# An adaLN block in float32 on one core: where the feed-forward takes its 64-row half block

## The chip, the cores and the metric

The kernel runs on 1 core of a Trainium2 chip. The metric is the device time of one execution in microseconds (us), lower is better. Three runs of the kernel before took 1242.53, 1242.93 and 1243.69 us; the median is 1242.93.

## What is computed

For each of 8 batches of 512 tokens with 1024 features, the reference computes (cut to what matters):

```python
mod = (silu(c) @ wmod)                      # shifts, scales and gates sa, ca, ga, sb, cb, gb
h = layernorm(x) * (1 + ca) + sa
x = x + ga * gelu(h @ ((w1.T @ w2.T) * sparse_mask) + b2)
h = layernorm(x) * (1 + cb) + sb
P = h @ U1                                  # 1024 -> 256
H = P @ V1 + b1                             # 256 -> 2 x 2752
act = silu(H[:, :2752]) * H[:, 2752:]       # gate half, up half
Z = act @ U2                                # 2752 -> 256
x = x + gb * (Z @ V2 + b2_ffn)              # 256 -> 1024
```

ga and gb are the gates, kept at a size of at least 0.25. All of it is in float32; the kernel splits each operand of a large product into a high and a low part and adds three products (hi x hi, hi x lo, lo x hi).

## The kernel before

It works in two passes. The first (until about 440 us) computes the modulation, the sparse attention-like product, the second normalisation and P, batch by batch, and stores x and P in HBM. The second pass is the feed-forward, one batch after the other, and the change is in it alone.

**Blocks.** The 2752 hidden features are taken in IB = 22 blocks: 21 of 128 and one of 64 (`width[-1]`, the half block). All five engines have their order written out by hand; semaphores tie them together. `three` (L498 to L500) issues the three matmuls of a split product. For a full block i TensorE computes

- the gate product (`gate_product`, 2 x 3 matmuls of 512 columns, into PSUM bank i % 2),
- the up product (`up_product`, as many, into bank 2 + i % 2),
- and, two blocks later, Z (`z_product`, 2 x 3 matmuls that add to banks 4 and 5).

For the half block, gate and up share one product of 6 matmuls (64 rows each in one bank). Its Z has only 64 rows to sum over, so the two column halves of U2 lie on different partitions and their matmuls run side by side on two halves of the array: 6 matmuls at L804, in three pairs, each a 64*128 tile of the array where all others are 128*128.

**Between the products.** ACT applies the silu (`silu`, L996) and writes the high part (`act_hi_part`, L1007; for the half block L1006 writes a second copy on the other 64 partitions first). DVE multiplies by up (`multiply`, L1285) and writes the low part (`act_lo_part`, L1295; for the half block L1293 first). ACT's order is silu of block i, then `act_hi` of block i - 1. DVE's is multiply of i, then `act_lo` of i - 1. Z of block i waits on `act_lo_ready`. The next gate product waits until the block before the last has been multiplied (`act_done`).

**The end of a batch.** TensorE's `batch` is

```python
            for i in range(2, IB):
                h_product(b, q, i)
                z_product(b, q, i - 2)
            if not last:
                gate_product(b + 1, 1 - q, 0)
            z_product(b, q, IB - 2)
            z_product(b, q, IB - 1)
            if not last:
                up_product(b + 1, 1 - q, 0)
                h_product(b + 1, 1 - q, 1)
            out_product(b)
```

so the next batch's first products lie between the last ones of this batch. After the last Z, ACT and DVE split Z (L1031, L1305) and the output product (`out_product`, 48 matmuls) follows. In the last batch there are no such products of a next batch.

**The V2 split.** V2 times the gate is split once per batch: ACT writes `v_hi` (L1014) in four parts, one after each of the `act_hi` parts of positions 12 to 15 (17 to 20 in batch 0), and GpSimd the four parts of `v_lo` (L1411) behind them.

**SP** issues all DMAs: P of the next batch behind a wait on `gate_done`, V2 and the broadcast gates behind waits on `v2_lo_ready` and `x2_biased`, and the output tiles and the next x tiles behind `out_ready`.

Of the kernel before, what the change touches and what calls it, by code (L numbers as in the profile page):

```python
# [30 lines left out]
ACT = mybir.ActivationFunctionType  # L31
ALU = mybir.AluOpType
AX = mybir.AxisListType

P = 128
# [4 lines left out]
def adaln_block(nc, x, w1, w2t, b2, mask, u1, v1, u2, v2, b1_main, b1_tail, b2f, ct, wmod, out):  # L40
    NB, TOK, D = x.shape
# [36 lines left out]
    with ExitStack() as ctx:  # L78
# [6 lines left out]
        bank = ctx.enter_context(nc.psum_tensor("bank", [P, 8, HALF], F32))  # L85


        b1_sb = buf(ctx, "b1_sb", [P, IB, 2])
# [68 lines left out]
        v1_hi = buf(p2, "v1_hi", [P, RB, 2 * INTER], F32R)  # L157
        v1_lo = buf(p2, "v1_lo", [P, RB, 2 * INTER], F32R)
# [8 lines left out]
        act = buf(p2, "act", [P, 2, TOK])  # L167
# [78 lines left out]
        gate_done = sem("gate_done")  # L246
# [44 lines left out]
        def at_start(b, early=True):  # L291

            return isinstance(b, int) and b == 0 and early
# [53 lines left out]
        BAND_ORDER = [6, 7] + list(range(6))  # L347
        V2_PARTS = [(r, slice(h * HALF, (h + 1) * HALF)) for r in range(RB) for h in range(NH)]
        V2_FROM = [17] + [12] * (NB - 1)

        block = ctx.enter_context(nc.Block())

# [142 lines left out]
        def _(pe):  # L495
# [252 lines left out]
            iteration(NB - 1, True, True, False)  # L748


            def h_waits(b, q, i):
                if i == 0:
                    pe.wait_ge(pt_in[q], (b - q) * 8 + 16)
                if not at_start(b, i < 2):
                    pe.wait_ge(act_done, b * IB + i - 1)

            def h_part(q, i, acc, name, v_hi, v_lo):
                if i % 4 == 0 or i == IB - 1:
                    pe.wait_ge(w_ready, piece_of[name, i // 4])
                for r in range(RB):  # L760
                    last = three(acc, v_hi[:, r], v_lo[:, r], pt[:, q, 0, r, :], pt[:, q, 1, r, :],
                                 r == 0, r == RB - 1)
                return last

            def gate_product(b, q, i):
                cols = slice(i * P, i * P + P)
                h_waits(b, q, i)
                h_part(q, i, bank[:, i % 2, :], "gate", v1_hi[:, :, cols], v1_lo[:, :, cols]).then_inc(gate_done, 1)

            def up_product(b, q, i):  # L770
                cols = slice(UP + i * P, UP + i * P + P)
                h_part(q, i, bank[:, 2 + i % 2, :], "up", v1_hi[:, :, cols], v1_lo[:, :, cols]).then_inc(up_done, 1)

            def h_product(b, q, i):

                if i < IB - 1:
                    gate_product(b, q, i)
                    up_product(b, q, i)
                else:
                    h_waits(b, q, i)  # L780
                    cols = slice(i * P, i * P + P)
                    h_part(q, i, bank[:, i % 2, :], "up", v1_hi[:, :, cols], v1_lo[:, :, cols]).then_inc(gate_done, 1)

            def z_product(b, q, i):
                pe.wait_ge(act_lo_ready, b * IB + i + 1)
                if i % 4 == 0:
                    pe.wait_ge(w_ready, piece_of["u2", i // 4])
                if at_start(b, i == 0):
                    pe.wait_ge(gb_ready, 1)
                elif i == 0:  # L790
                    pe.wait_ge(z_lo_ready, b * 2)
                w = width[i]
                slot = (q * IB + i) % 4
                if w == P:
                    for r in range(RB):
                        cols = slice(r * P, (r + 1) * P)
                        last = three(bank[:, 4 + r, :], u2_hi[:, i, cols], u2_lo[:, i, cols],
                                     act_hi[:, slot, :], act_lo[:, slot, :], i == 0, False)
                else:
                    terms = ((u2_hi, act_hi), (u2_hi, act_lo), (u2_lo, act_hi))  # L800
                    for t, (weight, moving) in enumerate(terms):
                        for r in range(RB):
                            rows = slice(r * w, (r + 1) * w)
                            last = nc.tensor.matmul(bank[:, 4 + r, :], weight[rows, i, r * P:(r + 1) * P],  # L804
                                                    moving[rows, slot, :], start=False, stop=t == len(terms) - 1)
                last.then_inc(z_step, 1)

            def out_product(b):
# [55 lines left out]
        def _(ae):  # L864
# [123 lines left out]
            iteration(NB, False, True, False)  # L988


            def silu(b, q, i):
                w = width[i]
                ae.wait_ge(gate_done, b * IB + i + 1)
                if not at_start(b, i < 2):
                    ae.wait_ge(act_lo_ready, b * IB + i - 1)
                nc.scalar.activation(act[0:w, i % 2, :], bank[0:w, i % 2, :], ACT.Silu,  # L996
                                     bias=b1_sb[0:w, i, 0:1]).then_inc(silu_done, 1)

            def act_hi_part(b, q, i):
                w = width[i]  # L1000
                slot = (q * IB + i) % 4
                ae.wait_ge(act_done, b * IB + i + 1)
                if not at_start(b, i < 4):
                    ae.wait_ge(z_step, b * IB + max(i - 3, 0))
                if w < P:
                    nc.scalar.activation(act_hi[w:P, slot, :], act[0:w, i % 2, :], ACT.Copy)  # L1006
                nc.scalar.activation(act_hi[0:w, slot, :], act[0:w, i % 2, :], ACT.Copy).then_inc(act_hi_ready, 1)  # L1007

            def v2_hi_part(b, part):
                r, cols = V2_PARTS[part]  # L1010
# [31 lines left out]
        def _(dve):  # L1042
# [229 lines left out]
            nc.vector.tensor_tensor(gbb2_rows, gb_rows[:], b2f_rows, ALU.mult).then_inc(gbb2_ready, 1)  # L1272


            def multiply(b, q, i):

                w = width[i]
                if w == P:
                    up = bank[0:w, 2 + i % 2, :]
                    dve.wait_ge(up_done, b * (IB - 1) + i + 1)  # L1280
                else:
                    up = bank[P - w:P, i % 2, :]
                    dve.wait_ge(gate_done, b * IB + i + 1)
                dve.wait_ge(silu_done, b * IB + i + 1)
                nc.vector.scalar_tensor_tensor(act[0:w, i % 2, :], up, b1_sb[0:w, i, 1:2],  # L1285
                                               act[0:w, i % 2, :], ALU.add, ALU.mult).then_inc(act_done, 1)

            def act_lo_part(b, q, i):
                w = width[i]
                slot = (q * IB + i) % 4  # L1290
                dve.wait_ge(act_hi_ready, b * IB + i + 1)
                if w < P:
                    nc.vector.tensor_tensor(act_lo[w:P, slot, :], act[0:w, i % 2, :], act_hi[0:w, slot, :],  # L1293
                                            ALU.subtract)
                nc.vector.tensor_tensor(act_lo[0:w, slot, :], act[0:w, i % 2, :], act_hi[0:w, slot, :],  # L1295
                                        ALU.subtract).then_inc(act_lo_ready, 1)

            def batch(b, q, last):
# [174 lines left out]
```

## Time and profile before

| | |
|---|---|
| median of three runs | 1242.93 us |
| the profiled execution: its time / its span | 1241.24 / 1239.5 us |
| busy: TensorE, weight load | 1186.1 us (96%), 950.3 us (77%) |
| busy: DVE, ACT, GpSimd | 669.8 (54%), 407.0 (33%), 314.9 us (25%) |
| granted TensorE clock, mean of the execution | 0.988 of full |
| HBM traffic over the span | 133 GB/s |

The span is the time between the first and last instruction of the profiled execution. Engines are PE (TensorE matmuls), PEld (its weight loads), DVE, ACT, POOL (GpSimd) and SP. A row of the timeline gives start and duration in us; matmuls overlap, so the distance of two starts tells more than the duration. In brackets stands how long the engine had been idle before and whose result ended that. The granted clock is 1.00 at 2.4 GHz and 0.50 at 1.2 GHz. In such rows x2 after a shape counts two instructions.

### The profile page before, as it was taken

Reading aid. Unit: us, or ns where it says so; the run is one execution under the profiler, and the core shown is the slowest. Engines: PE = TensorE matmul, PEld = TensorE weight load, DVE = VectorE, ACT = ScalarE, POOL = GpSimd, SP = SyncE. Lnnn points to the kernel's source line nnn. Section 1 sums busy time; section 2 is a strip of 40 time slices with the busy share of each in tenths; the row PEclk is TensorE's granted clock in tenths of the full one; section 3 lists DMA queues with packets and bytes.
Section 4 is the critical chain, followed back from the end, with each engine's and each line's share of the span. In section 5 each row is a group of like instructions: output and inputs, shape, how many; then the busy total and the mean of one; then the engine's idle time right before and its main releaser. Section 6 shows DMA issues by size and latency. Waiting matters only on the chain.

```text
span 1239.5 us, 15161 instructions
## 1 busy us (share of the span) xinstructions
PE 1186.1 (96%) x5617; PEld 950.3 (77%) x5617; DVE 669.8 (54%) x1049; ACT 407.0 (33%) x684; POOL 314.9 (25%) x257
## 2 busy tenths in 40 slices
PE   7788999999999899999999999999999999999997
PEld 4446678877786678888888888888888888888885
DVE  0838699999996643543444443443444444344343
ACT  0122334444443264413322323322332332332331
POOL 0023221332313176541211302203113122131110
PEclk9898999999999899999999999999999999999999
DMA  9796635535457454240131122104015014013001
GB/s 350 290 371 250 270 145 196 226 146 211 165 199 288 172 172 162 95 156 15 68 119 52 68 77 93 68 25 145 11 58 170 1 68 140 31 68 119 18 1 68
DMA packets 54145, 165.76 MB, mean 134 GB/s; under 512 B 4992, under 2 KB 9536, under 8 KB 52032
## 3 DMA queue, kind: packets, MB, share of 16 engines
q1 hardware_dynamic: 54080, 164.86, 36.3%
q8 instruction: 44, 0.72, 0.2%
q14 instruction: 21, 0.17, 0.0%
HBM read 122.84 MB, written 42.01 MB: 133 GB/s over the span
## 4 chain that ended last, share of the span: by engine, by line
PE 82%; DVE 9%; ACT 2%; issue 2%; DMA 2%; POOL 1%; SPq 1%; DVEq 0%; ACTq 0%
PE bank L498 25%; PE bank L500 24%; PE bank L499 24%; PE bank L568 4%; DVE nrm L1070 2%; PE bank L664 2%; DMA x<-in_x 2%; PE bank L533 2%; DVE bn L1228 1%; DVE h_lo L1171 1%; DVE bn L1060 1%; DMA wm_sb<-in_wmod 1%; POOL g L1349 1%; PE bank L804 1%; DVE xr L1223 1%
## 5 line engine op out<-in xcount | busy, mean ns | idle before, releaser
L1285 DVE SCALAR_TENSOR_TENSOR act<-bank,b_sb,act 128x512 f32<-128x512 f32 (+1 forms) x176 | 131.9, 750 | 382.4 <-PE bank L500 360.7
L996 ACT ACTIVATE act<-bank,b_sb 128x512 f32<-128x512 f32 (+1 forms) x176 | 121.1, 689 | 505.7 <-PE bank L500 504.5
L498 PE MATMUL bank<-pt,v_hi 128*128 128x512 f32 x688 | 268.7, 391 | 1.5 <-DVE act L1285 1.5
L499 PE MATMUL bank<-pt,v_hi 128*128 128x512 f32 x688 | 267.7, 389 | 0.0
L500 PE MATMUL bank<-pt,v_lo 128*128 128x512 f32 x688 | 267.7, 389 | 0.0
L1295 DVE TENSOR_TENSOR act_lo<-act,act_hi 128x512 fp32r<-128x512 f32 (+1 forms) x176 | 164.9, 937 | 0.2
L498 PEld LDWEIGHTS bank<-pt,v_hi 128*128 128x128 f32 x688 | 129.1, 188 | 31.2 <-issue 2.6
L500 PEld LDWEIGHTS bank<-pt,v_lo 128*128 128x128 f32 x688 | 129.2, 188 | 27.0
L499 PEld LDWEIGHTS bank<-pt,v_hi 128*128 128x128 f32 x688 | 129.2, 188 | 26.3
L1421 POOL TENSOR_TENSOR x2t<-gbb_bc,x2t 128x512 f32<-128x512 f32 x64 | 85.5, 1358 | 241.3 <-DMA x2t<-x_dram 241.3
L498 PE MATMUL bank<-act_hi,u_hi 128*128 128x512 f32 x336 | 130.8, 389 | 0.9 <-DVE act_lo L1295 0.9
L499 PE MATMUL bank<-act_lo,u_hi 128*128 128x512 f32 x336 | 130.7, 389 | 0.0
L500 PE MATMUL bank<-act_hi,u_lo 128*128 128x512 f32 x336 | 130.7, 389 | 0.0
L889 ACT ACTIVATE h_hi<-bank,now 128x512 fp32r<-128x512 f32 x128 | 84.6, 687 | 113.8 <-PE bank L568 113.6
L1171 DVE SCALAR_TENSOR_TENSOR h_lo<-bank,now,h_hi 128x512 fp32r<-128x512 f32 x128 | 92.7, 745 | 33.2 <-ACT h_hi L889 32.7
L1007 ACT ACTIVATE act_hi<-act 128x512 fp32r<-128x512 f32 (+1 forms) x176 | 109.5, 622 | 0.4 <-DVE act L1285 0.3
L1411 POOL TENSOR_TENSOR v_lo<-v2g,v_hi 128x512 fp32r<-128x512 f32 x32 | 41.4, 1295 | 244.1 <-ACT v_hi L1014 244.1
L1349 POOL TENSOR_TENSOR g<-g,now_ga 128x512 f32<-128x512 f32 x64 | 74.5, 1173 | 69.7 <-ACT g L894 61.8
L568 PE MATMUL bank<-ident,nrm 128*128 128x128 f32 x480 | 71.4, 282 | 12.6 <-DVE nrm L1070 9.0
L568 PEld LDWEIGHTS bank<-ident,nrm 128*128 128x128 f32 x480 | 57.2, 145 | 24.7 <-DVE h_lo L1171 8.7
L498 PE MATMUL bank<-h_hi,attn_hi 128*128 128x512 f32 x176 | 73.4, 417 | 2.5 <-DVE mod_sum L1133 2.2
L498 PEld LDWEIGHTS bank<-act_hi,u_hi 128*128 128x128 f32 x336 | 63.1, 188 | 14.4 <-DVE act_lo L1295 1.3
(122 smaller groups left out, 1600.2 us busy)
## 6 DMA issues: line engine op xcount, KB each, us to landing
wm_sb<-in_wmod SPq DMA_DIRECT2D x10, 2048.0 KB, 11.1
xr<-in_x SPq DMA_DIRECT2D x16, 1024.0 KB, 6.8
x_dram<-xr SPq DMA_DIRECT2D x16, 1024.0 KB, 4.2
x2t<-x_dram SPq DMA_DIRECT2D x32, 512.0 KB, 4.0
out<-x2t SPq DMA_DIRECT2D x32, 512.0 KB, 4.9
xs<-in_x SPq DMA_DIRECT2D x7, 2048.0 KB, 7.7
pt_dram<-pt_st SPq DMA_DIRECT2D x8, 1024.0 KB, 3.9
pt<-pt_dram SPq DMA_DIRECT2D x8, 1024.0 KB, 5.8
```

The lines of the kernel that those rows point to most:

```text
L498: nc.tensor.matmul(acc, s_hi, m_hi, start=start, stop=False)
L499: nc.tensor.matmul(acc, s_hi, m_lo, start=False, stop=False)
L500: return nc.tensor.matmul(acc, s_lo, m_hi, start=False, stop=stop)
L568: last = nc.tensor.transpose(bank[:, 2 + k % 2, n * P:(n + 1) * P], src[:, n, k * P:(k + 1) * P], ident[:])
L889: nc.scalar.activation(h_hi[:, k, :], bank[:, 2 + k % 2, :], ACT.Copy, scale=scale[:, k:k + 1]).then_inc(hi_ready, 1)
L996: nc.scalar.activation(act[0:w, i % 2, :], bank[0:w, i % 2, :], ACT.Silu, bias=b1_sb[0:w, i, 0:1]).then_inc(silu_done, 1)
L1007: nc.scalar.activation(act_hi[0:w, slot, :], act[0:w, i % 2, :], ACT.Copy).then_inc(act_hi_ready, 1)
L1171: nc.vector.scalar_tensor_tensor(h_lo[:, k, :], bank[:, 2 + k % 2, :], scale[:, k:k + 1], h_hi[:, k, :], ALU.mult, ALU.subtract).then_inc( ...
L1285: nc.vector.scalar_tensor_tensor(act[0:w, i % 2, :], up, b1_sb[0:w, i, 1:2], act[0:w, i % 2, :], ALU.add, ALU.mult).then_inc(act_done, 1)
L1295: nc.vector.tensor_tensor(act_lo[0:w, slot, :], act[0:w, i % 2, :], act_hi[0:w, slot, :], ALU.subtract).then_inc(act_lo_ready, 1)
L1349: nc.gpsimd.tensor_tensor(g[:, t, :], g[:, t, :], now_ga[:, t:t + 1].to_broadcast([P, TOK]), ALU.mult).then_inc(g_ready, 1)
L1421: nc.gpsimd.tensor_tensor(half, gbb2_bc[:, h * HALF:(h + 1) * HALF], half, ALU.add).then_inc(x2_biased, 1)
```

## The change

From batch 1 on, the half block is taken as the twelfth of 22: blocks 0 to 10, then block 21 (the half one), then 11 to 20. Batch 0 keeps the old order, since its weights arrive in that order. The functions of the three computing engines now get a position j and look up the block in `BLOCKS[b][j]`. Buffers and banks (j % 2, the slot of `act_hi`) and all semaphore counts go by position; weights and bias columns by block. `up_done` counts only full blocks, so its target comes from `whole_blocks`. The flag that closes the accumulation of Z moves to the last position.

```diff
+        BLOCKS = [list(range(IB))] + [list(range(IB // 2)) + [IB - 1] + list(range(IB // 2, IB - 1))] * (NB - 1)
+
+        def whole_blocks(b, j):
+            return b * (IB - 1) + sum(width[i] == P for i in BLOCKS[b][:j + 1])
...
-            def h_product(b, q, i):
-
-                if i < IB - 1:
-                    gate_product(b, q, i)
-                    up_product(b, q, i)
+            def h_product(b, q, j):
+                i = BLOCKS[b][j]
+                if width[i] == P:
+                    gate_product(b, q, j)
+                    up_product(b, q, j)
                 else:
-                    h_waits(b, q, i)
+                    h_waits(b, q, j)
...
-            def z_product(b, q, i):
-                pe.wait_ge(act_lo_ready, b * IB + i + 1)
+            def z_product(b, q, j):
+                i = BLOCKS[b][j]
+                pe.wait_ge(act_lo_ready, b * IB + j + 1)
...
-                                     act_hi[:, slot, :], act_lo[:, slot, :], i == 0, False)
+                                     act_hi[:, slot, :], act_lo[:, slot, :], j == 0, j == IB - 1)
...
-                    dve.wait_ge(up_done, b * (IB - 1) + i + 1)
+                    dve.wait_ge(up_done, whole_blocks(b, j))
```

`silu`, `act_hi_part`, `multiply` and `act_lo_part` change in the same way. The new lines shift line numbers: L804 becomes L812, L1285 becomes L1295, L1293 and L1295 become L1303 and L1305, L996 becomes L1006, L1006 and L1007 become L1016 and L1017, L498 to L500 become L503 to L505.

How the order of instructions moves is seen best at three places.

DVE at the end of batch 2, before (L1285 multiply, L1293 and L1295 `act_lo`, L1305 the split of Z):

```order
L1285 SCALAR_TENSOR_TENSOR act<-bank,b_sb,act 128x512
L1295 TENSOR_TENSOR act_lo<-act,act_hi 128x512
L1285 SCALAR_TENSOR_TENSOR act<-bank,b_sb,act 64x512
L1295 TENSOR_TENSOR act_lo<-act,act_hi 128x512
L1293 TENSOR_TENSOR act_lo<-act,act_hi 64x512
L1295 TENSOR_TENSOR act_lo<-act,act_hi 64x512
L1305 TENSOR_TENSOR z_lo<-bank,z_hi 128x512 x2
```

and now:

```order
L1295 SCALAR_TENSOR_TENSOR act<-bank,b_sb,act 128x512
L1305 TENSOR_TENSOR act_lo<-act,act_hi 128x512
L1295 SCALAR_TENSOR_TENSOR act<-bank,b_sb,act 128x512
L1305 TENSOR_TENSOR act_lo<-act,act_hi 128x512 x2
L1315 TENSOR_TENSOR z_lo<-bank,z_hi 128x512 x2
```

The two 64-row subtracts are gone from the end; two full ones stand behind a full multiply.

ACT in the middle of a batch, where the half block arrives, now (L1006 silu, L1016 and L1017 `act_hi`, L1024 `v_hi`):

```order
L1006 ACTIVATE act<-bank,b_sb 64x512
L1017 ACTIVATE act_hi<-act 128x512
L1006 ACTIVATE act<-bank,b_sb 128x512
L1016 ACTIVATE act_hi<-act 64x512
L1017 ACTIVATE act_hi<-act 64x512
L1024 ACTIVATE v_hi<-v2g 128x512
L1006 ACTIVATE act<-bank,b_sb 128x512
```

The two 64-row copies come just ahead of the first `v_hi`, in the place of one full copy.

TensorE in the middle of a batch, now: the last matmuls of the up product of position 13, the Z of the half block (L812) and the start of the gate product of position 14, with the semaphores waited on:

```order
L503 MATMUL bank<-pt,v_hi 128x512
L504 MATMUL bank<-pt,v_hi 128x512
L505 MATMUL bank<-pt,v_lo 128x512
L812 MATMUL bank<-act_hi,u_hi 128x512 [waits act_lo_ready]
L812 MATMUL bank<-act_hi,u_hi 128x512
L812 MATMUL bank<-act_lo,u_hi 128x512 x2
L812 MATMUL bank<-act_hi,u_lo 128x512 x2
L503 MATMUL bank<-pt,v_hi 128x512 [waits act_done]
```

Before, these six stood behind the Z of block 20 and ahead of the next batch's up product, at L804.

## Rows read from the trace of the kernel before

**Rows 1.** The page: busy us of each engine, share of the span, instructions.

```profile
PE 1186.1 (96%) x5617; PEld 950.3 (77%) x5617; DVE 669.8 (54%) x1049; ACT 407.0 (33%) x684; POOL 314.9 (25%) x257
```

**Rows 2.** Waits from 540 us on: who waited for whom, total us, times, longest.

```profile
PEld bank L804 <- DVE act_lo L1295: 5.1, 7, 0.9
...
PE bank L804 <- DVE act_lo L1295: 2.1, 7, 0.5
```

**Rows 3.** Timeline, end of batch 2: start us, us, engine, line, operation [idle before].

```profile
722.24 0.68 DVE L1295 TENSOR_TENSOR act_lo<-act,act_hi 64x512 fp32r<-64x512 f32 x1
722.31 0.39 PE L500 MATMUL bank<-act_hi,u_lo 128*128 128x512 f32 x1
...
722.98 0.50 PE L804 MATMUL bank<-act_hi,u_hi 64*128 64x512 f32 x2 [0.28 <-DVE act_lo L1295]
...
723.55 0.40 PE L804 MATMUL bank<-act_hi,u_lo 64*128 64x512 f32 x2
...
723.88 0.50 PE L498 MATMUL bank<-pt,v_hi 128*128 128x512 f32 x1
...
724.22 0.40 PE L499 MATMUL bank<-pt,v_hi 128*128 128x512 f32 x1
```

**Rows 4.** Timeline, TensorE at the end of batch 1.

```profile
623.60 0.49 PE L804 MATMUL bank<-act_hi,u_hi 64*128 64x512 f32 x2 [0.28 <-DVE act_lo L1295]
```

**Rows 5.** Timeline, end of the last batch: TensorE, ACT and DVE.

```profile
1211.50 0.69 ACT L996 ACTIVATE act<-bank,b_sb 128x512 f32<-128x512 f32 x1 [2.87 <-PE bank L500]
...
1213.80 0.39 PE L500 MATMUL bank<-act_hi,u_lo 128*128 128x512 f32 x1
...
1215.16 0.39 PE L500 MATMUL bank<-pt,v_lo 128*128 128x512 f32 x1
...
1215.58 0.69 ACT L996 ACTIVATE act<-bank,b_sb 64x512 f32<-64x512 f32 x1 [2.87 <-PE bank L500]
...
1216.17 0.62 ACT L1007 ACTIVATE act_hi<-act 128x512 fp32r<-128x512 f32 x1
...
1216.37 0.75 DVE L1285 SCALAR_TENSOR_TENSOR act<-bank,b_sb,act 64x512 f32<-64x512 f32 x1 [2.16 <-ACT act L996]
...
1217.05 0.68 DVE L1295 TENSOR_TENSOR act_lo<-act,act_hi 128x512 fp32r<-128x512 f32 x1
...
1217.15 0.63 ACT L1006 ACTIVATE act_hi<-act 64x512 fp32r<-64x512 f32 x1 [0.37 <-DVE act L1285]
...
1217.78 0.50 PE L498 MATMUL bank<-act_hi,u_hi 128*128 128x512 f32 x1 [0.87 <-DVE act_lo L1295]
...
1220.47 0.39 PE L804 MATMUL bank<-act_hi,u_lo 64*128 64x512 f32 x2
...
1222.88 0.50 PE L498 MATMUL bank<-v_hi,z_hi 128*128 128x512 f32 x1 [2.02 <-DVE z_lo L1305]
```

**Rows 6.** Timeline, first pass: TensorE goes to the 32-column form (L533) without a wait.

```profile
372.95 0.39 PE L500 MATMUL bank<-h_hi,attn_lo 128*128 128x512 f32 x1
...
373.27 1.92 PE L533 MATMUL bank<-xs,c_pad 128*32 128x512 f32 x16
```

**Rows 7.** Timeline, batch 1: GpSimd's `v_lo` and DVE's subtract beside it.

```profile
584.36 1.30 POOL L1411 TENSOR_TENSOR v_lo<-v2g,v_hi 128x512 fp32r<-128x512 f32 x1 [24.38 <-ACT v_hi L1014]
...
584.59 1.62 DVE L1295 TENSOR_TENSOR act_lo<-act,act_hi 128x512 fp32r<-128x512 f32 x1
```

**Rows 8.** Windows: us, busy PE, PEld, DVE, ACT, POOL, granted clock, DMA share, GB/s.

```profile
720.00:725.00 5.00, 4.72 (x23) 3.31 (x23) 2.54 (x5) 2.84 (x5) 0.00 (x0) 1.00 0.00 0
```

**Rows 9.** Window of the last output product, and two of its matmuls in the timeline.

```profile
1224.00:1225.00 1.00, 1.00 (x4) 0.80 (x3) 0.00 (x0) 0.00 (x0) 0.00 (x0) 0.50 0.00 0
...
1223.68 0.53 PE L498 MATMUL bank<-v_hi,z_hi 128*128 128x512 f32 x1
...
1227.33 0.39 PE L498 MATMUL bank<-v_hi,z_hi 128*128 128x512 f32 x1
```

More of the change, by code:

```diff
@@ L748, in _, with h_waits @@
             iteration(NB - 1, True, True, False)
-            def h_waits(b, q, i):
-                if i == 0:
+            def h_waits(b, q, j):
+                if j == 0:
                     pe.wait_ge(pt_in[q], (b - q) * 8 + 16)
-                if not at_start(b, i < 2):
-                    pe.wait_ge(act_done, b * IB + i - 1)
+                if not at_start(b, j < 2):
+                    pe.wait_ge(act_done, b * IB + j - 1)
             def h_part(q, i, acc, name, v_hi, v_lo):
@@ L804, in z_product @@
                             last = nc.tensor.matmul(bank[:, 4 + r, :], weight[rows, i, r * P:(r + 1) * P],
-                                                    moving[rows, slot, :], start=False, stop=t == len(terms) - 1)
+                                                    moving[rows, slot, :], start=False,
+                                                    stop=j == IB - 1 and t == len(terms) - 1)
                 last.then_inc(z_step, 1)
@@ L988, in _, with silu, act_hi_part @@
             iteration(NB, False, True, False)
-            def silu(b, q, i):
+            def silu(b, q, j):
+                i = BLOCKS[b][j]
                 w = width[i]
[L993 to L996, printed above, removed]
+                ae.wait_ge(gate_done, b * IB + j + 1)
+                if not at_start(b, j < 2):
+                    ae.wait_ge(act_lo_ready, b * IB + j - 1)
+                nc.scalar.activation(act[0:w, j % 2, :], bank[0:w, j % 2, :], ACT.Silu,
                                      bias=b1_sb[0:w, i, 0:1]).then_inc(silu_done, 1)
[L999 to L1004, printed above, removed]
+            def act_hi_part(b, q, j):
+                w = width[BLOCKS[b][j]]
+                slot = (q * IB + j) % 4
+                ae.wait_ge(act_done, b * IB + j + 1)
+                if not at_start(b, j < 4):
+                    ae.wait_ge(z_step, b * IB + max(j - 3, 0))
                 if w < P:
-                    nc.scalar.activation(act_hi[w:P, slot, :], act[0:w, i % 2, :], ACT.Copy)
-                nc.scalar.activation(act_hi[0:w, slot, :], act[0:w, i % 2, :], ACT.Copy).then_inc(act_hi_ready, 1)
+                    nc.scalar.activation(act_hi[w:P, slot, :], act[0:w, j % 2, :], ACT.Copy)
+                nc.scalar.activation(act_hi[0:w, slot, :], act[0:w, j % 2, :], ACT.Copy).then_inc(act_hi_ready, 1)
             def v2_hi_part(b, part):
@@ L1272, in _, with multiply, act_lo_part @@
             nc.vector.tensor_tensor(gbb2_rows, gb_rows[:], b2f_rows, ALU.mult).then_inc(gbb2_ready, 1)
-            def multiply(b, q, i):
+            def multiply(b, q, j):
+                i = BLOCKS[b][j]
                 w = width[i]
                 if w == P:
-                    up = bank[0:w, 2 + i % 2, :]
-                    dve.wait_ge(up_done, b * (IB - 1) + i + 1)
-                else:
[L1282 to L1291, printed above, removed]
+                    up = bank[0:w, 2 + j % 2, :]
+                    dve.wait_ge(up_done, whole_blocks(b, j))
+                else:
+                    up = bank[P - w:P, j % 2, :]
+                    dve.wait_ge(gate_done, b * IB + j + 1)
+                dve.wait_ge(silu_done, b * IB + j + 1)
+                nc.vector.scalar_tensor_tensor(act[0:w, j % 2, :], up, b1_sb[0:w, i, 1:2],
+                                               act[0:w, j % 2, :], ALU.add, ALU.mult).then_inc(act_done, 1)
+            def act_lo_part(b, q, j):
+                w = width[BLOCKS[b][j]]
+                slot = (q * IB + j) % 4
+                dve.wait_ge(act_hi_ready, b * IB + j + 1)
                 if w < P:
-                    nc.vector.tensor_tensor(act_lo[w:P, slot, :], act[0:w, i % 2, :], act_hi[0:w, slot, :],
+                    nc.vector.tensor_tensor(act_lo[w:P, slot, :], act[0:w, j % 2, :], act_hi[0:w, slot, :],
                                             ALU.subtract)
-                nc.vector.tensor_tensor(act_lo[0:w, slot, :], act[0:w, i % 2, :], act_hi[0:w, slot, :],
+                nc.vector.tensor_tensor(act_lo[0:w, slot, :], act[0:w, j % 2, :], act_hi[0:w, slot, :],
                                         ALU.subtract).then_inc(act_lo_ready, 1)
```

20 lines of the change are left out of this document (11 added, 9 removed).

## The prediction

> **What bounds the kernel now.** I read the page first: TensorE is busy for 1186.1 of 1239.5 us, the other engines for 54% or less [rows 1]. The change touches the feed-forward's batches 1 to 7 alone, from 540 us on. There the list of waits has only two entries that repeat and in which TensorE is the one that waits, both at L804, the product of the 64-row block: seven times, once a batch, for `act_lo` [rows 2]. Everything else in that list is another engine waiting for TensorE. So a saving on TensorE's queue in this stage comes through one for one, and a delay on ACT or DVE costs nothing until it holds a matmul back.
>
> The unit of the sum is one matmul of 512 columns. A full block has 18 (6 gate, 6 up, 6 Z), and 18 matmuls after one silu comes the next, 4.08 us on (1211.50 to 1215.58) [rows 5], so a **slot** is 4.08/18 = 0.227 us. A matmul's row is 0.39 long because matmuls overlap; what counts is the distance of starts. In the half block, the hidden product takes 6 slots and Z 3, since two 64-row matmuls run side by side (x2 in one row).
>
> What to see in [rows 3]: the end of a batch as it is. The last matmul of Z(20) starts at 722.31, so the next is due at 722.54. But L804 needs the second half of `act_lo`, which DVE starts at 722.24 and ends at 722.92; L804 starts at 722.98, 0.44 late. The next start is 0.34 behind it, 0.11 more than a slot (after any break the first row is 0.50 long, not 0.39). Leaving the two-tile form, 723.55 to 723.88 is 0.33 (0.10 over), and 723.88 to 724.22 again 0.34 (0.11 over). Sum: 0.44 + 0.11 + 0.10 + 0.11 = **0.76 us per batch over its slots**. Cross-check: from one L804 to the next is 722.98 - 623.60 = 99.38 us [rows 3, 4]; a batch has 21 x 18 + 9 + 48 (output) = 435 slots, 98.60 us, which leaves 0.78.
>
> The last batch has no next batch's products as cover [rows 5]. From 1213.80 (last start of Z(18)) to 1220.47 (last pair of Z(21)) are 6.67 us for 21 slots (4.76): **1.91 us over**. Z(20) waits too, because `act_hi`(20) stands on ACT behind the silu of the short block and `act_lo`(20) on DVE behind its multiply. Then Z is split and the output product starts at 1222.88.
>
> **The change, part by part.** No instruction is added or removed; 7 of 8 batches (1 to 7) take the half block as their twelfth, and a full one last. Slots, bytes, DMAs and the numbers of ACT and DVE operations stay. Batch 0 keeps its order and its 0.76.
>
> 1. *Wait at the end of batches 1 to 6.* With a full block last, its up product ends 18 slots (Z(19), the next gate, Z(20)), 4.08 us, before its Z is due. From the last start of up to a usable `act_lo`, by the steps of [rows 5]: 0.42 to DVE's start, 0.78 to `act_hi`, 0.65 more (0.62 and the signal), 0.68 subtract, 0.06 to TensorE = 2.6 us. It fits by 1.5, and Z(20) by more. Removed: the whole 0.76, as no form switch is left there either.
>
> 2. *The switch of form is not removed but moved.* In the middle, nothing waits (part 3), but the array still goes from 128-row to 64-row matmuls and back. The way out is read above, 0.10 + 0.11. The way in without a wait is not in the feed-forward. The nearest row is the switch to the 32-column form in the first pass, where no engine is waited for [rows 6]: 372.95 to 373.27 is 0.32, 0.09 over. I take 0.09 + 0.11 for the way in; together 0.41 us per batch. Bounds: from below 0 (the switch is hidden by weights loaded ahead), from above the 0.44 + 0.11 of today, if what looks like a wait were the switch. I take the value of [rows 6], as the idle of L804 is put down to DVE and the 0.06 from the end of `act_lo` to the start fits a signal.
>
> The Trainium skill, "TensorEngine Tiling (Array Packing)", under "Key Properties", says that a change of tiling mode (not of tile) drains TensorE. By a full drain the next matmul would start 0.39 behind the last, 0.16 over instead of 0.09, and the sum below would be about 0.5 us smaller over seven batches. The row at 373.27, 0.32 behind its predecessor, speaks against the full price, though not against the rule.
>
> Saved in batches 1 to 6: 0.76 - 0.41 = 0.35 each, **2.1 us**.
>
> 3. *Does the wait come back in the middle?* Take T as the last start of the short hidden product. ACT runs silu, then `act_hi` of the block before; DVE multiply at T + 1.21. The next silu is due only when the next gate is complete, 12 slots on: T + 2.72 + 0.42 = 3.14, and both `act_hi` halves follow by 5.0. DVE starts the next multiply at T + 4.50 (18 slots and 0.42) and the two `act_lo` halves at 5.2 and 5.9, done by 6.6. TensorE wants them after 36 slots, T + 8.16. One thing crosses: the V2 split begins at this very position, and where GpSimd computes `v_lo` a DVE subtract takes 1.62 instead of 0.68 [rows 7]. Even with both halves at 1.62 the chain ends at 5.2 + 3.2 = 8.4, and the first pair is due at T + 8.39 plus 0.09. So: nothing, at worst 0.1. Z of the block before the half block has 18 slots between the end of the short product and its own start, as in any step. SP's order is unchanged: its waits on `gate_done` 22 per batch count the same, and `v2_lo` comes 6 slots earlier in the batch, before loads that are used a batch later.
>
> 4. *The last batch.* With G the last start of the last block's gate: silu at G + 0.42, `act_hi`(20) done at G + 1.63; up's last start G + 1.36, multiply at G + 1.78, `act_lo`(20) from G + 2.46 to 3.14 (0.68 behind the multiply's start, as 1217.05 behind 1216.37), Z(20) at G + 3.19. It is due 13 slots on, at G + 2.95: 0.24 late, and 0.11 for the restart. `act_lo`(21) is ready by G + 4.0, Z(21) due at 4.7: no wait. Over slots: 0.35 at the end and 0.41 in the middle, 0.76 for 1.91 today. Saved: **1.15 us**. Behind it the chain is the same: last start of Z to first output matmul 2.41 us.
>
> Sum: 2.1 + 1.15 = 3.25, say **3.2 us less**. The profiled execution has a span of 1239.5 and a time of 1241.24; its span would be 1236.3. The median of the runs shown is 1242.93, 1.7 above, and the forecast goes from it: **1239.7 us**. About 0.2% (2.5 us) is what a measurement of this kernel can tell from no change.
>
> **Rivals.**
> - *The way in costs in the middle what it costs now* (0.44 + 0.11). Then batches 1 to 6 save nothing and the last 1.91 - 0.35 - 0.76 = 0.8: 1242.1 us. For it: the waits are 2.1 us over seven with 0.5 as the longest [rows 2], so they hardly differ from batch to batch, as a fixed price would. Against it: [rows 6], and that a chain of ACT and DVE steps of fixed length is as even.
> - *The low clock goes too.* In the last output product the granted clock falls from 2.4 to 1.2 GHz after TensorE had been idle for 2.0 us and, before that, in two breaks of 0.9 [rows 5] and 0.5 [rows 2]; the window from 1224 shows 0.50 [rows 9]. Nine starts from 1223.68 take 3.65 us instead of 2.04, which costs 1.6. The change takes most of the two earlier breaks away and leaves the 2.0. If the fall needs them: 3.2 + 1.6 = 4.8 less, 1238.1 us. I hold it unlikely, as the longest break stays.
> - *A wait takes the place at the batch's end*: the last full block comes later than the short one, and if GpSimd is at work there each subtract takes 1.62. In batches 1 to 6 this would cost at most 0.1, and in the last batch, where Z(20) would come at G + 4.1, 1.3 late with its restart, it leaves next to nothing (1.91 - 1.45 - 0.41), since Z(21) would be 0.15 late as well. With 2.1 - 0.6 from the others some 1.6 less, 1241.3 us. Against it: in the 5 us around the end of batch 2 GpSimd does nothing [rows 8].
> - *Slower*: the half block meets the V2 split in the middle, ACT and DVE fall behind and TensorE waits at L804 there, where it costs 0.35 per batch before anything is lost. It decides when the chain of part 3 ends later than T + 8.8; for 2.5 us of loss it must end 0.8 us past the due time in all seven batches, at T + 9.3: 1245.4 us. Rows give 8.4 at worst.
>
> **How the numbers follow.** Forecast 0.62 (its own range 1238.9 to 1240.6, of which about 0.07 falls within 0.2%), way in at today's price 0.14, clock 0.12, wait at the end 0.08, slower 0.04. Faster by over 0.2%, that is under 1240.4: 0.55 + 0.12 = 0.67. Within: 0.07 + 0.14 + 0.08 = 0.29. Slower: 0.04. The range of 8 in 10 is 1238.0 to 1242.0: it ends just past the clock case and just short of the first rival, and leaves out the slow case and about half of each of those two (0.04 + 0.06 + 0.07). The bounds of the way in are its bounds too: free, it would save 7 x 0.2 more (1238.3); at today's price it is the first rival.
>
> **What would show it.** Right: L804 in batches 1 to 7 without idle put down to DVE, its first start about 0.32 behind the matmul before it; 99.03 us from one batch to the next where it was 99.38; one late Z(20) of about 0.24 in the last batch; 2.0 us of idle before the output product still there. Wrong: the distance of 0.67 stays at L804 in the middle (first rival), a clock of 1.00 throughout the last 20 us (second), idle before Z(20) in batches 1 to 6 (third), or over 0.7 us at L804 (fourth).

## The result, and the profile after

| | before | changed |
|---|---|---|
| median, 9 runs each | 1242.6 us (1241.32 to 1243.69) | 1239.13 us (1238.01 to 1239.99) |
| profiled execution: time / span | 1241.24 / 1239.5 us | 1238.43 / 1236.6 us |
| TensorE busy | 1186.1 us | 1185.6 us |

The ratio is 0.9971, with a 95% interval of 0.9960 to 0.9981. That is 3.5 us less, with an interval of some 2.4 to 5.0. It is 0.29% faster; the weak end of the interval, 0.19%, lies just short of the 0.2% that the prediction set as its line. Forecast were 3.2 us less, 1239.7 us.

The waits from 540 us on, in the changed kernel (who waited for whom, total us, times, longest). They answer to [rows 2]:

```profile
DVE z_lo L1315 <- ACT z_hi L1041: 26.5, 7, 3.9
...
ACT act L1006 <- DVE act_lo L1305: 15.0, 7, 2.4
...
PEld bank L812 <- issue: 2.5, 7, 0.4
...
PE bank L503 <- DVE z_lo L1315: 2.0, 1, 2.0
...
PEld bank L503 <- DVE act_lo L1305: 0.5, 1, 0.5
```

The half block's Z (now L812) waits for nobody any more in batches 1 to 7: its weight load is put down to "issue". The 2.0 us ahead of the last output product are still there.

TensorE in the middle of batch 1 and of batch 2:

```profile
586.55 0.39 PE L505 MATMUL bank<-pt,v_lo 128*128 128x512 f32 x1
586.87 0.50 PE L812 MATMUL bank<-act_hi,u_hi 64*128 64x512 f32 x2
587.20 0.40 PE L812 MATMUL bank<-act_lo,u_hi 64*128 64x512 f32 x2
587.44 0.39 PE L812 MATMUL bank<-act_hi,u_lo 64*128 64x512 f32 x2
587.76 0.50 PE L503 MATMUL bank<-pt,v_hi 128*128 128x512 f32 x1
588.10 0.40 PE L504 MATMUL bank<-pt,v_hi 128*128 128x512 f32 x1
...
685.90 0.50 PE L812 MATMUL bank<-act_hi,u_hi 64*128 64x512 f32 x2
```

The way in is 0.32 (586.55 to 586.87) where it was 0.67 in [rows 3]; then 0.33, 0.24, 0.32 and 0.34. The five distances make 1.55 us; five slots are 1.13, so the visit (into the 64-row form and out again) costs 0.42 us. From L812 to L812 are 685.90 - 586.87 = 99.03 us, where [rows 3, 4] had 99.38.

ACT and DVE around the half block in batch 2:

```profile
683.41 1.68 DVE L1305 TENSOR_TENSOR act_lo<-act,act_hi 64x512 fp32r<-64x512 f32 x1
...
685.19 0.69 ACT L1006 ACTIVATE act<-bank,b_sb 128x512 f32<-128x512 f32 x1 [2.10 <-DVE act_lo L1305]
...
686.01 0.75 DVE L1295 SCALAR_TENSOR_TENSOR act<-bank,b_sb,act 128x512 f32<-128x512 f32 x1 [0.92 <-PE bank L505]
```

GpSimd works beside the second half's subtract (its `v_lo` starts at 683.16 and takes 1.39), and the subtract takes 1.68 us and ends at 685.09; the pair is at 685.90. The silu of position 13 waits for that subtract, since it overwrites the same `act` buffer, and starts some 0.5 us late; DVE's next multiply at 686.01 still waits for TensorE alone, so nothing is lost.

The end of a full batch, batch 2: no break in TensorE's queue, with the last Z product and the next batch's up product a slot apart. Z(21) starts at 722.29, and the last `act_lo` was ready at 720.56.

```profile
719.08 1.48 DVE L1305 TENSOR_TENSOR act_lo<-act,act_hi 128x512 fp32r<-128x512 f32 x2
...
722.29 0.39 PE L503 MATMUL bank<-act_hi,u_hi 128*128 128x512 f32 x1
...
723.42 0.39 PE L505 MATMUL bank<-act_hi,u_lo 128*128 128x512 f32 x1
723.65 0.39 PE L503 MATMUL bank<-pt,v_hi 128*128 128x512 f32 x1
```

And the last batch (it answers to [rows 5]):

```profile
1210.44 0.39 PE L505 MATMUL bank<-act_hi,u_lo 128*128 128x512 f32 x1
...
1214.52 0.39 PE L505 MATMUL bank<-act_hi,u_lo 128*128 128x512 f32 x1
1214.99 0.50 PE L503 MATMUL bank<-act_hi,u_hi 128*128 128x512 f32 x1
1215.34 0.40 PE L504 MATMUL bank<-act_lo,u_hi 128*128 128x512 f32 x1
...
1217.66 0.39 PE L505 MATMUL bank<-act_hi,u_lo 128*128 128x512 f32 x1
1220.06 0.50 PE L503 MATMUL bank<-v_hi,z_hi 128*128 128x512 f32 x1 [2.01 <-DVE z_lo L1315]
```

Z(20) starts at 1214.99 where 1214.75 was due, 0.24 late, with 0.12 for the restart; Z(21) follows without a gap. The output product starts 2.40 us behind the last start of Z, as before (2.41).

**The stretch.** Runs of one kernel differ by a us or two, and much of that arises ahead of batch 1, where only two of the versions below, all_batches and halves, differ from the others (the first matmul after batch 0's output product starts at 540.20 before and 540.54 now). So below I also compare the *stretch*: from that matmul's start to the last matmul's start. The changed kernel was traced twice (changed_again, part 4): the spans are 1236.6 and 1235.6 us, the stretches 691.92 and 691.93. All others but full_rows were traced once.

In the kernel before:

```profile
540.20 0.39 PE L498 MATMUL bank<-pt,v_hi 128*128 128x512 f32 x1
...
1235.28 0.39 PE L500 MATMUL bank<-v_hi,z_lo 128*128 128x512 f32 x1
```

In the changed kernel:

```profile
540.54 0.39 PE L503 MATMUL bank<-pt,v_hi 128*128 128x512 f32 x1
...
1232.46 0.39 PE L505 MATMUL bank<-v_hi,z_lo 128*128 128x512 f32 x1
```

695.08 us before, 691.92 now: 3.16 us less, for 3.25 in the sum of the prediction. Both include the fall of the clock at the end (part 4).

### The profile page after: what moved, and what is told of

The parts are those of the page before. It is cut to its first block, busy times and chain, and to the rows that moved or that the text cites. A ratio compares the mean times of both kernels' runs of the same rounds, so it can differ in the third digit from the quotient of the medians.

```text
span 1236.6 us, 15161 instructions
## 1 busy us (share of the span) xinstructions
PE 1185.6 (96%) x5617; PEld 950.3 (77%) x5617; DVE 666.6 (54%) x1049; ACT 408.4 (33%) x684; POOL 316.9 (26%) x257
## 4 chain that ended last, share of the span: by engine, by line
PE 84%; DVE 8%; DMA 2%; issue 2%; ACT 1%; SPq 1%; POOL 1%; DVEq 0%; ACTq 0%
PE bank L503 25%; PE bank L505 25%; PE bank L504 25%; PE bank L573 4%; DVE nrm L1080 2%; PE bank L669 2%; PE bank L538 2%; DMA x<-in_x 2%; DVE bn L1238 1%; DVE h_lo L1181 1%; DVE bn L1070 1%; DMA wm_sb<-in_wmod 1%; POOL g L1359 1%; DVE xr L1233 1%; PE bank L812 1%
## 5 line engine op out<-in xcount | busy, mean ns | idle before, releaser
L1295 DVE SCALAR_TENSOR_TENSOR act<-bank,b_sb,act 128x512 f32<-128x512 f32 (+1 forms) x176 | 132.0, 750 | 372.8 <-PE bank L505 349.8
L1006 ACT ACTIVATE act<-bank,b_sb 128x512 f32<-128x512 f32 (+1 forms) x176 | 121.2, 690 | 495.2 <-PE bank L505 478.9
L503 PE MATMUL bank<-pt,v_hi 128*128 128x512 f32 x688 | 269.1, 391 | 1.5 <-DVE act L1295 1.5
L505 PE MATMUL bank<-pt,v_lo 128*128 128x512 f32 x688 | 268.0, 390 | 0.0
L1305 DVE TENSOR_TENSOR act_lo<-act,act_hi 128x512 fp32r<-128x512 f32 (+1 forms) x176 | 161.6, 918 | 0.9
L503 PEld LDWEIGHTS bank<-pt,v_hi 128*128 128x128 f32 x688 | 129.2, 188 | 31.5 <-DVE act L1295 4.1
L505 PEld LDWEIGHTS bank<-pt,v_lo 128*128 128x128 f32 x688 | 129.2, 188 | 26.6
L503 PE MATMUL bank<-act_hi,u_hi 128*128 128x512 f32 x336 | 131.0, 390 | 0.1
L505 PE MATMUL bank<-act_hi,u_lo 128*128 128x512 f32 x336 | 130.9, 390 | 0.0
L1017 ACT ACTIVATE act_hi<-act 128x512 fp32r<-128x512 f32 (+1 forms) x176 | 109.8, 624 | 7.0 <-DVE act L1295 6.9
L503 PE MATMUL bank<-h_hi,attn_hi 128*128 128x512 f32 x176 | 73.1, 415 | 2.5 <-DVE mod_sum L1143 2.2
L503 PEld LDWEIGHTS bank<-act_hi,u_hi 128*128 128x128 f32 x336 | 63.1, 188 | 13.6 <-DVE act_lo L1305 0.5
```

Source lines behind the costliest of these rows:

```text
L503: nc.tensor.matmul(acc, s_hi, m_hi, start=start, stop=False)
L505: return nc.tensor.matmul(acc, s_lo, m_hi, start=False, stop=stop)
L1006: nc.scalar.activation(act[0:w, j % 2, :], bank[0:w, j % 2, :], ACT.Silu, bias=b1_sb[0:w, i, 0:1]).then_inc(silu_done, 1)
L1017: nc.scalar.activation(act_hi[0:w, slot, :], act[0:w, j % 2, :], ACT.Copy).then_inc(act_hi_ready, 1)
L1295: nc.vector.scalar_tensor_tensor(act[0:w, j % 2, :], up, b1_sb[0:w, i, 1:2], act[0:w, j % 2, :], ALU.add, ALU.mult).then_inc(act_done, 1)
L1305: nc.vector.tensor_tensor(act_lo[0:w, slot, :], act[0:w, j % 2, :], act_hi[0:w, slot, :], ALU.subtract).then_inc(act_lo_ready, 1)
```

## The experiments

All stretches are worked out from such pairs of rows. A ratio is to executions of the kernel before that were timed together with that version; their median moved from 1241.5 to 1242.6 us, so the medians of different rows can't be compared closely.

| run | stretch, us | against changed | median, us | ratio to before, 95% interval |
|---|---|---|---|---|
| before | 695.08 | +3.16 | | |
| changed | 691.92, 691.93 | | 1239.13 | 0.9971 (0.9960 to 0.9981) |
| last_only | 694.03 | +2.11 | 1239.55 | 0.9984 (0.9975 to 0.9993) |
| inner_only | 693.00 | +1.08 | 1239.81 | 0.9986 (0.9977 to 0.9995) |
| three_switches | 697.75 | +5.83 | 1243.9 | 1.0016 (1.0007 to 1.0026) |
| full_rows | 692.06, 693.64 | see below | 1240.4, 1241.98 | one execution each |
| second_last | 692.49 | +0.57 | 1238.66 | 0.9974 (0.9963 to 0.9986) |
| fifth | 691.93 | +0.01 | 1238.98 | 0.9976 (0.9965 to 0.9986) |
| filled | 690.30 | -1.62 | 1236.52 | 0.9962 (0.9949 to 0.9976) |
| before_filled | 693.56 | +1.64 | 1240.35 | 0.9986 (0.9976 to 0.9996) |
| all_batches | 690.32 | -1.60 | 1237.53 | 0.9960 (0.9946 to 0.9974) |
| halves | 689.53 | -2.39 | 1237.02 | 0.9959 (0.9945 to 0.9973) |

**1. Which places give the gain?** Two kernels with one part of the change each. last_only:

```diff
-        BLOCKS = [list(range(IB))] + [list(range(IB // 2)) + [IB - 1] + list(range(IB // 2, IB - 1))] * (NB - 1)
+        BLOCKS = [list(range(IB))] * (NB - 1) + [list(range(IB // 2)) + [IB - 1] + list(range(IB // 2, IB - 1))]
```

> Theory (the gain is the sum of seven places): only the last batch gets the half block in its middle, so only its 1.15 us are saved against the kernel before, ratio about 0.999, span about 1238.3; batches 1 to 6 keep 99.38 us from one half block to the next. Rival (all of the gain comes out of the end of the program, where the chain is bare): nearly the whole 3.5 us, span about 1236.

inner_only:

```diff
-        BLOCKS = [list(range(IB))] + [list(range(IB // 2)) + [IB - 1] + list(range(IB // 2, IB - 1))] * (NB - 1)
+        BLOCKS = [list(range(IB))] + [list(range(IB // 2)) + [IB - 1] + list(range(IB // 2, IB - 1))] * (NB - 2) + [list(range(IB))]
```

> Theory: six times 0.35 = 2.1 us less than the kernel before, ratio about 0.9983, span about 1237.4; 99.03 us from one half block to the next in batches 1 to 6, and the last batch ends as before, with 1.91 us over its slots. Rival (gain only at the end of the program): no change.

Measured in the stretch: 695.08 - 694.03 = 1.05 us from the last batch, 695.08 - 693.00 = 2.08 us from the six others; together 3.13, the whole gain of 3.16. In last_only the old wait stands in batches 1 to 6 (six times; the last batch has none):

```profile
PE bank L812 <- DVE act_lo L1305: 1.7, 6, 0.3
```

The rival falls: batches 1 to 6 give two thirds. The timed ratios (0.9984 and 0.9986) each exclude 1 and cannot tell the two parts from each other; the stretch can. The span of last_only, 1239.1 us, was above the 1238.3 expected, as its first pass took 0.75 us more (540.95 against 540.20).

**2. What does a visit to the 64-row form cost?** three_switches takes the pairs apart:

```diff
                     for t, (weight, moving) in enumerate(terms):
+                        if b and t == 1:
+                            gate_product(b, q, j + 3)
+                        elif b and t == 2:
+                            up_product(b, q, j + 3)
...
                 for i in range(2, IB):
-                    h_product(b, q, i)
+                    if not (b and i == IB // 2 + 3):
+                        h_product(b, q, i)
                     z_product(b, q, i - 2)
```

> As the changed kernel, but the three pairs of 64-row matmuls in batches 1 to 7 stand apart, with the gate and the up product of the position after next between them: three visits to the 64-row form instead of one. Theory (a visit costs 0.41 us: 0.09 + 0.11 in, 0.10 + 0.11 out): two more visits per batch, 7 x 0.82 = 5.7 us more than the changed kernel, about 1244.9 us. Rival (the switch is nearly free and 0.41 was something else at the place): within 0.5 us of the changed kernel.

Its middle of batch 1:

```profile
587.15 0.39 PE L505 MATMUL bank<-pt,v_lo 128*128 128x512 f32 x1
587.47 0.50 PE L816 MATMUL bank<-act_hi,u_hi 64*128 64x512 f32 x2
587.90 0.50 PE L503 MATMUL bank<-pt,v_hi 128*128 128x512 f32 x1
588.23 0.39 PE L504 MATMUL bank<-pt,v_hi 128*128 128x512 f32 x1
```

A pair alone costs 0.32, 0.43 and 0.33, which is 1.08 for three slots (0.68): 0.40. Two more visits in seven batches cost 5.83 us, 0.42 each. The rival falls. The timed ratio, 1.0016, is slower than before: two more visits outweigh what the moved wait gives.

full_rows does without the form. It takes the weights of block 0 there, so it leaves the half block's right share out of Z, and serves for its times alone:

```diff
-                            rows = slice(r * w, (r + 1) * w)
-                            last = nc.tensor.matmul(bank[:, 4 + r, :], weight[rows, i, r * P:(r + 1) * P],
-                                                    moving[rows, slot, :], start=False,
+                            last = nc.tensor.matmul(bank[:, 4 + r, :], weight[:, 0, r * P:(r + 1) * P],
+                                                    moving[:, slot, :], start=False,
```

> As the changed kernel, but the Z of the half block is done with six 128-row matmuls, on weights of block 0 and all 128 rows of act, so the half block's share of Z is not what the reference asks for; there is no change of form. Theory: three more slots (0.68) and no visit to the 64-row form (0.41) per batch: 0.27 us more in each of batches 1 to 7, 99.30 us from batch to batch, 1.9 us more in the stretch from batch 1 to the end. Rival (a visit costs as much as the old wait and its breaks, 0.76): 0.1 us less per batch.

Its six matmuls in two batches:

```profile
588.40 0.39 PE L505 MATMUL bank<-pt,v_lo 128*128 128x512 f32 x1
588.63 0.62 PE L811 MATMUL bank<-act_hi,u_hi 128*128 128x512 f32 x2
...
687.91 0.62 PE L811 MATMUL bank<-act_hi,u_hi 128*128 128x512 f32 x2
```

The way in is 0.23, a plain slot, and from batch to batch are 687.91 - 588.63 = 99.28 us for 99.30 expected. So doing the half block side by side is worth 0.25 us net in each batch (99.28 - 99.03): 0.68 us for the three slots saved, less 0.42 for the visit. The stretch of this first run, 692.06, is not 1.9 longer than the changed kernel's but 0.14, and the reason is the clock (part 4).

**3. Does it have to be the middle?** second_last puts the half block at position 20, fifth at position 4:

```diff
+        BLOCKS = [list(range(IB))] + [list(range(IB - 2)) + [IB - 1, IB - 2]] * (NB - 1)
...
+        BLOCKS = [list(range(IB))] + [list(range(4)) + [IB - 1] + list(range(4, IB - 1))] * (NB - 1)
```

> The half block as the last but one of batches 1 to 7, not in the middle. Theory (what counts is how many slots lie between a block's hidden product and its Z): in batches 1 to 6 the Z of the half block is still covered (its act_lo ready at G + 3.9, the pair due at G + 4.3), so 99.03 us from batch to batch as with the middle; in the last batch the pair is due at G + 2.95 and 0.96 late, so 1.28 us over its slots at the end where the changed kernel has 0.76 in all: 0.5 us more than the changed kernel. Rival (it must stand in the middle, away from the end): batches 1 to 6 wait at the half block again, 2 us more than the changed kernel.

> The half block as the fifth of batches 1 to 7, away from the V2 split, which stays at positions 12 to 15. Theory (the split beside it costs nothing, as the pair was due 0.8 us after act_lo): the same stretch from batch 1 to the end as the changed kernel, 691.9 us, within 0.1. Rival (DVE's 1.68 us subtract beside GpSimd holds something back): up to 0.5 us less.

second_last: in batches 1 to 6 the pair stands 0.32 behind its predecessor (720.79 to 721.11), as in the middle. In the last batch it waits for `act_lo`:

```profile
1214.62 0.39 PE L505 MATMUL bank<-act_hi,u_lo 128*128 128x512 f32 x1
1215.90 0.50 PE L812 MATMUL bank<-act_hi,u_hi 64*128 64x512 f32 x2 [0.90 <-DVE act_lo L1305]
```

1.05 us late where 0.96 was worked out; the stretch is 0.57 longer than the changed kernel's, for 0.5. So what counts is how many slots lie between a block's hidden product and its Z, not the place as such, and only the last batch makes a difference. fifth: 691.93 against 691.92. The V2 split beside the half block costs nothing, and the rival (up to 0.5) falls.

**4. The clock at the end.** filled puts work into the idle, before_filled does so in the kernel before:

```diff
                     h_product(b + 1, 1 - q, 1)
+                else:
+                    for n in range(9):
+                        nc.tensor.matmul(bank[:, n % 2, :], v1_hi[:, 0, 0:P], pt[:, q, 0, 0, :],
+                                         start=True, stop=True)
                 out_product(b)
```

> As the changed kernel, with nine more matmuls of 512 columns into idle banks after the last Z of the last batch, where TensorE is idle for 2.0 us while Z is split; their results are not used. Theory (the fall of the clock follows from that idle): granted clock 1.00 through the last output product, 1.6 us less than the changed kernel, about 1237.5 us. Rival (the fall has another cause, or comes anyway): no change, clock 0.50 for some 3.4 us as before; if nine matmuls reach past the end of the split, up to 0.3 us more.

> The kernel before with nine unused matmuls in the 2.0 us of idle ahead of the last output product. Theory (this idle alone makes the clock fall; the breaks of 0.9 and 0.5 us ahead of it do not): granted clock 1.00 in the output product, 1.6 us less than before. Rival (the earlier breaks make it fall, in whole or in part): the clock falls all the same, no change.

Windows of the changed kernel (us, then busy PE, PEld, DVE, ACT, POOL, granted clock, DMA share, GB/s):

```profile
1221.00:1222.00 1.00, 1.00 (x4) 0.81 (x3) 0.00 (x0) 0.00 (x0) 0.00 (x0) 0.50 0.00 0
1222.00:1223.00 1.00, 1.00 (x4) 0.81 (x3) 0.51 (x1) 0.00 (x0) 0.00 (x0) 0.50 0.00 0
1223.00:1224.00 1.00, 1.00 (x4) 0.71 (x4) 0.18 (x1) 0.00 (x0) 0.00 (x0) 0.50 0.00 0
```

and of filled, with the unused matmuls in its timeline:

```profile
1221.00:1222.00 1.00, 1.00 (x6) 0.80 (x5) 0.54 (x1) 0.00 (x0) 0.00 (x0) 1.00 0.00 0
1222.00:1223.00 1.00, 1.00 (x6) 0.84 (x5) 0.33 (x2) 0.00 (x0) 0.00 (x0) 1.00 0.00 0
```

```profile
1217.59 2.20 PE L845 MATMUL bank<-pt,v_hi 128*128 128x512 f32 x9
1219.77 0.50 PE L503 MATMUL bank<-v_hi,z_hi 128*128 128x512 f32 x1
```

The clock stays at 2.4 GHz, and the stretch is 1.62 us shorter (1.6 expected). In before_filled it stays there as well, although the breaks of 0.9 and 0.5 us remain:

```profile
1225.00:1226.00 1.00, 1.00 (x6) 0.84 (x5) 0.69 (x1) 0.00 (x0) 0.00 (x0) 1.00 0.00 0
```

695.08 - 693.56 = 1.52 less. So those breaks alone did not bring the fall in this one trace, and the changed kernel, where all but 0.24 us of them is gone, had it in both of its traces.

But the idle of 2.0 us doesn't always bring it either. The first trace of full_rows has the same idle and no fall. Hence two repeats.

> full_rows once more, unchanged (the half block's share of Z is again computed on other weights). In its first trace the granted clock stayed at 1.00 through the last output product although TensorE had been idle for 2.01 us ahead of it, as in the kernels where it fell. Theory (the idle makes the fall possible, and whether it comes changes from one execution to the next): the clock may fall this time, and then the stretch from batch 1 to the end is 1.6 us longer, 693.7 us. Rival (something in this kernel's end keeps the clock up): 1.00 again, 692.1 us.

> The changed kernel once more, unchanged. Theory (from one execution to the next): the stretch from batch 1 to the end is 691.9 us with a fall of the clock or about 690.3 without. Rival (this kernel's end always makes the clock fall): 691.9 us again.

One window of each of the two executions of full_rows, the first and the second:

```profile
1226.00:1230.00 4.00, 4.00 (x19) 3.29 (x19) 1.97 (x4) 0.00 (x0) 0.00 (x0) 1.00 0.32 131
```

```profile
1226.00:1230.00 4.00, 4.00 (x14) 3.19 (x13) 1.12 (x3) 0.00 (x0) 0.00 (x0) 0.69 0.14 56
```

19 matmuls against 14, in one kernel, with 2.01 us of idle ahead in both. The stretch is 692.06 without the fall and 693.64 with it. The second, against the changed kernel's 691.92 (also with a fall), gives 1.72 us for the 1.9 expected of full_rows; the first, against filled (no fall in either), gives 692.06 - 690.30 = 1.76. changed_again had the fall again: 539.48 to 1231.41 is 691.93 us. There it begins elsewhere, too:

```profile
1219.01 0.74 PE L503 MATMUL bank<-v_hi,z_hi 128*128 128x512 f32 x1 [2.01 <-DVE z_lo L1315]
1219.55 0.63 PE L504 MATMUL bank<-v_lo,z_hi 128*128 128x512 f32 x1
```

The second start of the output product is already 0.54 behind the first; in the first trace of the same kernel these are 0.33, and the starts grow apart only from the third on (1220.62, 1220.97, 1221.40). So in the last output product no fall was seen where the idle was filled; where it was left, whether the fall comes and when it begins differ between executions. The fall came in all eight other traces with this idle left bare (before, changed twice, last_only, inner_only, second_last, fifth, three_switches) and in one of the two of full_rows. What decides stays open.

**5. Faster than both kernels.** all_batches is filled with the half block second to last in batch 0 too (`BLOCKS` begins with `list(range(IB - 2)) + [IB - 1, IB - 2]`). halves adds a split of the last Z in two halves of 256 tokens:

```diff
+        def z_parts(last):
+            return [slice(0, TOK // 2), slice(TOK // 2, TOK)] if last else [slice(0, TOK)]
...
-                for r in range(RB):
-                    dve.wait_ge(z_hi_ready, b * 2 + r + 1)
-                    nc.vector.tensor_tensor(z_lo[:, r, :], bank[:, 4 + r, :], z_hi[:, r, :],
-                                            ALU.subtract).then_inc(z_lo_ready, 1)
+                for part, toks in enumerate(z_parts(last)):
+                    for r in range(RB):
+                        dve.wait_ge(z_hi_ready, b * 2 + part * RB + r + 1)
+                        nc.vector.tensor_tensor(z_lo[:, r, toks], bank[:, 4 + r, toks], z_hi[:, r, toks],
+                                                ALU.subtract).then_inc(z_lo_ready, 1)
```

ACT's split goes likewise, with a wait on `z_lo_ready` before each step of the second half, so that the two engines never read one bank at once.

> The changed kernel with two additions: batch 0 takes the half block as its last but one as well, and nine unused matmuls fill the 2.0 us of idle ahead of the last output product. Theory: 1.6 us less for the clock; in batch 0 the 0.76 us over the slots become 0.41 (0.35 less), unless the last weight pieces come too late for it. Together 1.95 us less than the changed kernel, about 1237.2 us. Rival for batch 0 (the up piece of the weights holds the half block back one position earlier): nothing, or a loss, there.

> As all_batches, but in the last batch Z is split in two halves of 256 tokens, so that the output product can start when the first half is split, with six unused matmuls in the gap. Theory: from the last start of Z to the first output matmul 1.7 us instead of 2.41, as each of the first ACT and DVE steps is near half as long; the second half of the split is done beside the output product's first four blocks: 0.7 us less than all_batches, granted clock 1.00. Rival (the steps have a fixed cost, and ACT and DVE take turns on the two banks): under 0.3 us.

all_batches: batch 0 is 0.32 us shorter (from its first Z matmul to the end of its output product 541.25 - 444.88 = 96.37, for 540.54 - 443.85 = 96.69 in the changed kernel; 0.35 expected), the rest as filled (stretch 690.32 against 690.30). Its median is 1237.53 us for about 1237.2 expected. halves at its end:

```profile
1216.83 0.39 PE L508 MATMUL bank<-act_hi,u_lo 128*128 128x512 f32 x1
1217.06 1.52 PE L850 MATMUL bank<-pt,v_hi 128*128 128x512 f32 x6
1217.26 0.66 ACT L1053 ACTIVATE z_hi<-bank 128x256 fp32r<-128x256 f32 x2 [3.04 <-PE bank L508]
1217.67 1.63 DVE L1329 TENSOR_TENSOR z_lo<-bank,z_hi 128x256 fp32r<-128x256 f32 x4 [2.73 <-ACT z_hi L1053]
...
1218.48 0.50 PE L506 MATMUL bank<-v_hi,z_hi 128*128 128x512 f32 x1
```

1.65 us from the last start of Z to the output product, where it was 2.40; the stretch is 0.79 shorter than all_batches' (0.7 expected). It has the shortest stretch of all, with a median of 1237.02 us and a ratio of 0.9959 (0.9945 to 0.9973) to the kernel before. The timed intervals of halves, all_batches and filled overlap, and with 5 runs each they can't be told from one another, only from before.

## Why the prediction was right

- *The wait at the batch's end goes whole.* Right: no break from Z(21) to the next up product. The sum gave 1.5 us of slack; the rows show 1.7 (720.56 to 722.29).
- *The switch of form is moved, not removed, at 0.41 us.* Right, and the step with the least to stand on: the way in was taken from a different switch in the first pass, 0.09 over a slot; measured 0.32 - 0.23 = 0.09. That two different changes of form cost the same was partly luck, since no row of the kernel before showed the one in question without a wait. With the breaks behind it, 0.42 per visit, confirmed by tripling the visits (0.42 each) and by doing without them. The Trainium skill, "TensorEngine Tiling (Array Packing)", "Key Properties", says that a change of tiling mode drains TensorE. The rows agree in so far as every change of form has its break and full_rows has none. The next matmul starts 0.32 behind the last and not 0.39, so the full price that the prediction tried is too high; but 0.39 is a modelled length, and what makes the 0.09 was not shown.
- *2.1 us from batches 1 to 6.* Measured 2.08.
- *1.15 us from the last batch.* Measured 1.05 in last_only. From the rows above: from the last start of Z(18) (1210.44) to 1217.66 are 7.22 us for 30 slots (6.80), 0.42 over for the 0.35 of the sum, as some starts behind a break are 0.23 to 0.24 apart instead of 0.227. With 0.42 for the visit that is 0.84 over the slots, where 0.76 was forecast. Z(20) was late by exactly the 0.24 worked out.
- *Nothing waits in the middle.* Right for TensorE: `act_lo` was ready at 685.09, 0.8 us ahead of the pair. The prediction's bound, with both subtracts at 1.62, left next to no slack; only the second one was slow. It didn't name the silu of position 13, which overwrites the half block's `act` buffer and starts 0.5 us late. That was covered as well, by the up product.
- *The forecast of the median.* 3.2 less forecast, 3.5 measured with an interval of 2.4 to 5.0. The stretch says 3.16; the rest isn't told apart from the scatter ahead of batch 1. The forecast went from a median of 1242.93 in three runs, which was 1242.6 in nine.
- *What bounds it.* The prediction calls every other entry of the list of waits an engine that waits for TensorE. That is wrong in the wording: the list also has waits for ACT and for DMAs, and TensorE itself waits twice at the program's end (0.9 and 2.0 us). The conclusion holds, since in none of these does TensorE wait in batches 1 to 6.
- *Rivals.* The way in at today's price: refuted by the 0.32. A wait in place of the old one: only the 0.24 of the last batch. Slower: refuted by fifth, where moving away from the V2 split changes nothing. The clock: the fall stayed, as forecast, and before_filled and the changed kernel's two traces speak against the earlier breaks as its cause; but my reason, that it follows from the longest break, was too simple, since one execution of full_rows had the break and not the fall. The prediction of the median didn't hang on it, though the sum took a fall on both sides for granted.

## What to carry to other kernels

Where work is handed round three engines two steps behind, count for each block the matmul slots between its own product and the one that needs the result: a short block has the longest chain (two copies and two subtracts here) and makes the cover of its neighbours short, so it should not stand last, and in a batch with nothing behind it not last but one either (0.57 us worse here). Price what moves along with it: a change of array form costs the same wherever it stood here, and only the wait is saved. And for differences of one us in a run of 1240, compare a stretch of the trace between two instructions of the bound engine, not the medians alone.

## What I had not expected of the hardware

- The same program with the same 2.01 us of TensorE idle had the granted clock fall to 0.50 in one execution and stay at 1.00 in another; it is worth 1.6 us in the last output product. It stayed at 1.00 in all three traces with nine unused matmuls in the gap (filled, before_filled, all_batches) and in the one of halves with six.
- Leaving the 64-row form costs as much as entering it, 0.1 us at the change and 0.11 at the next start, and a pair of matmuls that stands alone between two changes pays both (0.32, 0.43, 0.33 against 0.227 a slot).
- A DVE subtract that starts beside GpSimd's `v_lo` takes 1.68 us instead of 0.68, also for 64 rows instead of 128.
